# Sending three tiles per block to the expert regions, from the fifth block on, in place of one

## What is computed

```python
def step(S, inp):                      # 512 steps, one after the other
    k_t, q_t, v_t, beta_t, a_t = inp
    S = S * a_t[..., None, None]
    kv_mem = einsum('bhd,bhde->bhe', k_t, S)
    delta = (v_t - kv_mem) * beta_t
    S = S + k_t[..., :, None] * delta[..., None, :]
    y_t = einsum('bhd,bhde->bhe', q_t, S)
    return (S, y_t)
...
x = layernorm(x + attention(x))
e = argmax(x @ router_w.T)             # one expert of 8 for each token
y = down[e] @ (silu(gate[e] @ x) * (up[e] @ x))
x = layernorm(x + y)
```

## Time and profile before

| | us |
|---|---|
| median of 3 runs | 808.16 (805.93 to 808.61) |
| span of the profiled execution | 808.6 |
| DVE busy | 630.6 (78%) |
| PE busy | 689.3 (85%) |
| POOL busy | 642.0 (79%) |
| ACT busy | 414.5 (51%) |
| TensorE's mean granted clock, share of full | 0.912 |

### The profile page before, as it was taken

One profiled execution on the slowest core, in us unless ns is written; L12 is line 12 of the kernel. 1 busy time (PEld: TensorE's weight loads), 2 busy tenths in 40 slices (PEclk: granted clock), 3 DMA queues, 4 the chain that ended last, 5 costly groups with the idle time before them and its releaser, 6 DMA issues.

```text
span 808.6 us, 13837 instructions
## 1 busy us (share of the span) xinstructions
PE 689.3 (85%) x3545; PEld 516.8 (64%) x3545; DVE 630.6 (78%) x1697; ACT 414.5 (51%) x1281; POOL 642.0 (79%) x789
## 2 busy tenths in 40 slices
PE   8679788998999989899899995977775769999991
PEld 3436465566756657566575564756665769999890
DVE  3899999999999999999999999899611524666430
ACT  6635555457564575645656455232231245666561
POOL 2989999899999999999999999987537334444574
PEclk9989999999999999999999997878677789999996
DMA  6823234333343332443333422064433355767630
GB/s 171 206 75 94 82 103 115 87 81 98 94 116 102 82 97 80 110 121 82 89 88 110 109 69 82 17 199 143 158 109 116 119 170 184 244 231 235 224 109 8
DMA packets 135918, 97.27 MB, mean 120 GB/s; under 512 B 95630, under 2 KB 110225, under 8 KB 135714
## 3 DMA queue, kind: packets, MB, share of 16 engines
q1 hardware_dynamic: 130514, 87.55, 36.7%
q0 software_dynamic: 4320, 8.43, 3.2%
q10 hardware_dynamic: 1008, 0.43, 0.2%
HBM read 39.80 MB, written 31.43 MB: 88 GB/s over the span
## 4 chain that ended last, share of the span: by engine, by line
DVE 36%; PE 34%; POOL 13%; issue 5%; ACT 4%; another core or an unknown queue 4%; SPq 1%; DMA 1%; POOLq 0%; DVEq 0%; ACTq 0%
PE banks L433 10%; PE banks L689 7%; DVE banks L1852 6%; DVE upd L1840 6%; DVE banks L1826 5%; PE banks L446 5%; DVE prod L1810 4%; POOL q_prod L1290 4%; DVE banks L1836 4%; DVE mix L1830 4%; DVE upd L1821 3%; PE banks L742 2%; POOL u L1290 2%; PE banks L674 1%
## 5 line engine op out<-in xcount | busy, mean ns | idle before, releaser
L1290 POOL TENSOR_TENSOR q_prod<-s_keep,q_gam 128x512 f32<-128x512 f32 x128 | 139.9, 1097 | 12.8 <-ACT s_keep L1000 11.8
L742 PE MATMUL banks<-q_prod,ident 128*128 128x256 f32 x496 | 119.6, 397 | 23.8 <-POOL q_prod L1290 23.6
L1000 ACT ACTIVATE s_keep<-banks 128x128 f32<-128x128 f32 x128 | 49.8, 389 | 158.5 <-DVE upd L1840 158.5
L742 PEld LDWEIGHTS banks<-q_prod,ident 128*128 128x128 f32 x496 | 96.1, 199 | 49.0 <-POOL q_prod L1290 35.7
L433 PE MATMUL banks<-xs_t,w_tile 128*128 128x128 f32 x852 | 114.1, 284 | 13.0 <-ACT xs_t L463 5.2
L542 POOL DMA_INDIRECT out<-rows_out,xs x71 | 70.0, 986 | 59.7 <-ACT rows_out L523 53.2
L433 PEld LDWEIGHTS banks<-xs_t,w_tile 128*128 128x128 f32 x852 | 106.0, 199 | 16.4 <-issue 9.3
L1852 DVE TENSOR_REDUCE banks<-upd 128x128 f32<-128x640 f32 x127 | 105.1, 827 | 7.6 <-DVE upd L1840 0.5
L577 DVE TENSOR_TENSOR hid<-banks,silu 128x384 f32<-128x384 f32 x71 | 39.6, 558 | 89.6 <-PE banks L433 36.3
L689 PE MATMUL banks<-kkqk,ident 128*128 128x320 f32 (+2 forms) x272 | 88.6, 488 | 9.9 <-ACT y_rms L1028 5.3
L1826 DVE TENSOR_REDUCE banks<-prod 128x64 f32<-128x576 f32 x128 | 93.7, 732 | 0.0
(11 more groups left out here) (219 smaller groups left out, 1459.9 us busy)
## 6 DMA issues: line engine op xcount, KB each, us to landing
w_tile<-gate_up_we SPq DMA_DIRECT2D x71, 352.0 KB
xs<-x_sorted SPq DMA_DIRECT2D x71, 64.5 KB
x_ct<-in_x_ct SPq DMA_DIRECT2D x16, 256.0 KB, 3.0
k_dram<-kq_s SPq DMA_DIRECT2D x16, 256.0 KB, 3.0
q_dram<-kq_s SPq DMA_DIRECT2D x16, 256.0 KB, 3.7
out<-v_s SPq DMA_DIRECT2D x16, 256.0 KB, 2.7
out<-beta SPq DMA_DIRECT2D x16, 256.0 KB, 2.6
k_h<-k_dram SPq DMA_DIRECT2D x16, 256.0 KB
```

The costliest lines, as they stand in the source:

```text
L742: i = mm(out, ident[:, :], q_prod[m][:, :, d, :], start=(m == 0 and d == 0), stop=(d == DH - 1), skip_group_check=True)
L1290: b.step(label, win, lambda: tt(out, x, y, op))
```

## The change

SORTED gives three tiles to every block from 4 to 14, where it gave one to the blocks 4 to 13 and three to block 14. Block 15 sends 13 tiles as before, with numbers higher by 20. The tail sends 18 (46 to 63) where it sent 38 (26 to 63): 6, 4 and 8 in place of 10, 4 and 24. The number of transfers is the same.

```diff
-        SORTED = {w: max(w - 4, 0) for w in range(-2, NW - 2)}
-        SORTED.update({NW - 2: 10, NW - 1: 13})
+        SORTED = {w: max(3 * (w - 4), 0) for w in range(-2, NW)}
...
             if b.tail:
                 w0 = SORTED[w - 1] + 13
                 q_times_s(p, NCH - 1)
-                sort_to(w0, w0 + 10)
+                sort_to(w0, (NW - 3) * TW)
                 context(p)
-                sort_to(w0 + 10, w0 + 14)
+                sort_to((NW - 3) * TW, (NW - 2) * TW)
                 b.wait(act, "ln_ln", p)
                 mul("ln_r", p, rstd[:, :], rstd[:, :], minus_half[:, :].to_broadcast([P, TW]), ALU.pow)
-                for win in range((w0 + 14) // TW, NW):
-                    sort_to(max(w0 + 14, win * TW), (win + 1) * TW)
+                sort_to((NW - 2) * TW, (NW - 1) * TW)
+                sort_to((NW - 1) * TW, NW * TW)
                 return
```

## The result

The changed kernel takes 813.45 us (median of five runs, 812.25 to 815.87) beside 805.93 for the kernel before (five runs, 803.31 to 808.61). The ratio is 1.0079, with a 95% interval of 1.0050 to 1.0109: slower by some 0.8%. The profiled span grew from 808.6 to 813.7 us, by 5.1.

A forecast was written before the change was run, and what follows sets the result against it. DVE and POOL were taken as full, DVE held through POOL's ring. Span 808.6 + 22.5 (blocks: 19.5 + 3 clock) - 12.8 (hand-over) = 818.3, so 818 by the runs' median; forecast's own range 812 to 824, wider range 810 to 829.

The forecast's parts named there:

- The blocks' price: Blocks 4 to 13: twenty added transfers at 1.22 us on POOL, less 4.9 us of its waits, cost 19.5 us.
- The clock: Blocks 4 to 13: longer PE idle time lowers TensorE's clock and slows lines 742 and 689; +3 us, bounds 0 to 15.
- Where DVE waits: Changed blocks: DVE's kkd waits for PE's line 689, about 2.4 us in each block.
- A transfer beside a busy DVE: In the blocks: 0.05 us more per transfer by the rows, 1 us in all; by the skill's port rule 50 us.
- The first lot: Hand-over: six transfers in place of ten let y_rms follow PE's sums at once; -3 us, 0 to -4.
- The late ln_r and the stall: Hand-over, third lot: ln_r 8.6 us later behind four transfers, but the stall before tile 5's hid goes; net -9.8 us.
- Rival 2: Hand-over: stall not the lots' doing, or short lots stall as long; gain 0 to 4, 829 us; 0.17 with (3), (4).

The follow-up runs named there:

- ln_r first: The changed kernel with ln_r moved ahead of the wait and the four transfers of tiles 52 to 55; 810.69 us, 0.9982 of the kernel before.
- the spaced third lot: The kernel before with one POOL product behind each pair of transfers 40 to 51; 804.52 us, 0.9921 of the kernel before.
- 16 products: The changed kernel with 16 POOL products into a scratch tile between ln_r and the transfers of tiles 56 to 63; 1.0364 of the kernel before.
- the first lot spaced: The kernel before with the first lot's ten transfers in pairs, one POOL product between pairs, third lot still 24 long; 1.0004 of the kernel before.
- 16 indirect transfers: The changed kernel with 16 more indirect transfers into an unread spare tensor, between ln_r and the transfers of tiles 56 to 63; 1.0350 of the kernel before.

## Why the prediction was right

I forecast 818, 10 us more than before; the median is 813.45, 7.5 us more than before (in the profiled spans 5.1 more), and slower by 0.8%. Most of the mechanism came as forecast. My sum for the spans was +9.7, and these terms make it +5.1: the clock's 3 us didn't come, the hand-over gave 1.5 us more, and the blocks 14 and 15 gave 1.7 us that I had at nothing; 1.35 us that aren't the change's, and 0.2 in phase B, went the other way. Step by step:

**The blocks' price: right, and to the tenth by luck.** From q_prod7 of block 3 (162.35) to that of block 13 (520.66) it is 358.3 us against 338.8 (161.0 to 499.79): +19.5, as worked out from 20 x 1.22 less 4.9 of waits. The changed kernels agree among themselves: 357.8 to 358.6 in all eight traces. Those with one transfer a block don't: they take 335.2 to 338.8, since a period without the added transfers is 33.4 us in some blocks and 34.05 in others, and which ones differs from trace to trace. So the price is 19.5 to 23 us, and the trace that I read lies at one end. In seven further runs with these blocks the last q_prod7 stands at 590 to 594, at either level.

**The clock: mis-sized.** I added 3 us; it was 0. The granted clock did fall (0.91 for 0.95 in block 6, 0.85 for 0.93 in block 13), but the period stayed at 35.8: POOL no longer waits for kkd, so what PE loses doesn't reach it. My range's upper end (34.5 for the blocks) rested on this term alone.

**Where DVE waits: wrong place, right amount.** I expected 2.4 us a block at kkd. The waits make 2.1 a block, but only 2.1 us in ten blocks at kkd; the rest is at the router's count of tokens (line 1567) and at d_keep, ACT's copy of a chunk (line 1851).

**A transfer beside a busy DVE: by the row.** The mean of all 64 on POOL is 994 ns and the longest 1146. The 50 us that I had estimated from the Trainium skill (SBUF — State Buffer, section "Who interferes with whom") didn't come. I had misapplied the rule. That section names copies, casts and tensor_scalar as what can take the pair, and reports that tensor_tensor and tensor_reduce did not stall such transfers. In the ten changed blocks these two are 378 of the 386 us that DVE is busy, so the trace agrees with the page.

**The first lot: right.** y_rms came 4.0 us earlier by its place (3 forecast, 0 to 4).

**The late ln_r and the stall: right in kind, each a little off.** I had the stall go and ln_r come late, net -9.8 at tile 5; with the first lot -12.8. Measured -15.5 at tile 5 and -14.3 at phase B. The stall went as I argued (3.0 us between tiles 4 and 5). ln_r came 2.5 us later than before, counted from the last q_prod7, and not 5.6 (8.6 less the first lot's 3): the four transfers that wait for block 13's place start 28.8 us behind it, where I had reckoned with 31.6 (34.6 less 3). What the order costs against ln_r first is close to my 8.6: tile 17 comes 7.7 us earlier with ln_r first at the 807 level. At the 780 level it is 8.7 earlier (80.9 to 72.2) between two kernels that differ in their lots as well.

**Rival 2 (the stall isn't the lots' doing) is refuted at the 807 level** by the spaced third lot, and it would be the right account at the 780 level, where there is no stall for short lots to remove. There kernels with the changed blocks and with ln_r late took 1.031 to 1.036 of the kernel before. The changed kernel itself wasn't run at that level. What was added to these three stands behind ln_r, where it moved nothing up to tile 17, so I expect 1.036 for it, as for the one with 16 products, which has no spare tensor: 19.5 us for the blocks and 8.7 for ln_r, with no stall to set against them. That is argued, not measured. So the sum that came out at +5 (and at +8 when both kernels ran again) holds for one level; in the other the same steps make over 20. My text took the stall for a property of the kernel; it is one of the kernel and of circumstances of the measurement that I can't name.

**What stays open.** What differs between the levels isn't shown. The same chip gave both. In the rows of the hand-over it is "issue" and "remote" waits of ACT, of DVE and of PE's matmuls; at the 780 level DVE has none there, ACT at most 0.7 us and PE 0.2. The DMA engines weren't full (0.20), so the share of the 16 DMA engines in the Trainium skill (DMA: Bandwidth & Descriptors, section "Issuing engines are not separate DMA queues") doesn't explain it.

One difference between the levels I had overlooked: the traces of the 807 level lack records. The profile gives a landing time for the rows that POOL scatters to out in all seven traces of the 780 level, and in none of the seven of the 807 level. The kernel before, run again, and its version with the first lot spaced:

```profile
out<-rows_out,xs POOLq DMA_INDIRECT x71
out<-rows_out,xs POOLq DMA_INDIRECT x71, 3.1
```

From the last q_prod7 to tile 17 the first of these traces holds 644 semaphore updates by DMAs, for 102 transfers, and the second 1530, for 97; up to 161 us both hold 1540. So an "issue" or "remote" of the 807 level can be a usual wait whose releaser wasn't recorded. ACT's y_sq in the changed kernel (807 level), and in the one with 16 indirect transfers (780 level), 9.1 us behind the last q_prod7 in both:

```profile
602.95 0.60 ACT L1020 ACTIVATE y_sq<-banks 128x512 f32<-128x512 f32 x1 [7.33 <-issue]
602.90 0.60 ACT L1036 ACTIVATE y_sq<-banks 128x512 f32<-128x512 f32 x1 [7.35 <-PE banks L770]
```

The wait is the same and only its name is lost. That the stalls are real stands on the places (tile 5 at 55.6 against 32.3) and on the times of the executions, not on these names. Whether what loses the records also holds the engines up, so that the stall belongs to the recording and not to the kernel, no run tested.

## What to carry to other kernels

Work moved onto an engine that is already full in a loop costs its length less that engine's own waits, whatever it relieves elsewhere; read the waits, not the busy share. When a stage begins with a short operation of a busy engine (here ln_r), put everything else behind it: that alone was worth 8 us at the 807 level; at the other it wasn't tested alone. Before a stall is taken as a kernel's own, run the kernel before again and look whether the stall is still there: here it came and went from one measurement to the next, and with it some 27 us.

## What I had not expected of the hardware

The kernel before takes 779 to 780 us or 806 to 811, and all kernels of one measurement share the level. At the higher one the other engines stand still beside an unbroken row of indirect transfers from POOL, in the traces that lack records. In the kernel before, run again, DVE waited 30.3 us for "issue" and "remote", ACT up to 9.2 us for "remote" at one instruction, and PE 11.6 us for "issue" in the matmuls of the router and its count (part of these waits can be usual ones without a name). Sixteen in a row put tile 5 18 us later, twelve made a pause of 12.7 us; pairs with a product of 1.05 us between them did neither. At the lower level 24 in a row cost nothing. Most of the difference stands between the last q_prod7 and tile 17: 99.4 us in the kernel before at the higher level, and 72.3 at the lower one in its version with the first lot spaced, which has the same third lot and takes the time of the kernel before. Another 5 us stand behind tile 17 (138.4 us to the end against 133.2).
